# A scanned early-fusion layer on one core: pixel norm moved behind the embedding, text feed-forward blocks split over two loop bodies, feed-forward weights prepared ahead of the scan

## The chip, the cores and the metric

One core of a Trainium2 chip. The metric is the device time of one execution, in microseconds, as the median of several runs. Before: 1290.85 us, median of 3 runs (1287.31 to 1292.6). Engines are named as the profile names them: PE (TensorE), DVE (VectorE), ACT (ScalarE), POOL (GpSimd), SP (SyncE, which here only issues DMAs).

## The reference, cut to what matters

```python
h = tok(x)                 # 32 images, 14x14 patches of 16x16x3 -> 256: pixel layernorm with gain and
                           # bias, @ W (768x256) + bias, layernorm with gain and bias
h = concatenate([h, txt])  # 196 + 77 = 273 tokens of 256, batch 32
# scan over every second token (TIMESCALE = 2), D = 256, S = 64
x_sub = rmsnorm(layernorm(h)[:, ::2]) * g_norm
x_proj, gate = split(x_sub @ w_in.T + b_in)
def step(s, xt):
    s = tanh(s * A + xt[:, :, None] * Bm)      # s: 32 x 256 x 64
    return s, s @ Cm.sum(0) + Dv * xt
attn = (scan(step, x_proj) * silu(gate)) @ w_out.T + b_out
h = h + repeat(attn, 2)
f = layernorm(h)
h = h + (silu(f @ wg.T) * (f @ wu.T)) @ wd.T   # int weights / 127, hidden 768
```

## The kernel before

**Tiling.** The 273 tokens are cut into 20 groups of 14 rows (one row of patches, or 14 text tokens; the last has 7): 14 image groups, then 6 text groups. A group gives 7 scan steps (4 in the last). The state of the scan (256 x 64 per batch element, 32 elements) is held as 8 chunks of 128 x 512 in a ring `h`. So a group is 56 slots of one chunk each: DVE grows the chunk (`grow`, L829: old state times A into one of four PSUM banks `U`), PE adds the input (`drive`, L1384, with weights `b_st` and moving `x_diag`), ACT takes the tanh back into `h` (`squash`, L1097). In a slot the growth waits for the squash four slots earlier. After each step PE sums the state into `Y` (`read_step`, L1394).

**Bodies.** One loop body `i` does five things at once, of five groups: loads and normalises the pixels of group `r = i+1` (`ahead`), embeds, normalises and projects group `g = i` (`pre`), scans `s = i-1` (`scan`), takes `q = i-2` through attention output, residual and the feed-forward blocks (`post`), and does the down projection and output of `d = i-3` (`down`). Bodies -1 to 2 are unrolled, 3 to 12 are a loop of image bodies, 13 is the last image body, 14 to 18 a loop of text bodies, 19 the last one, 20 to 22 are the tail: body 20 has the last 32 scan slots.

**Order.** Each engine runs its own stream. What it does beside the scan is written out by hand in `PLANS`: for each kind of body, each part has the slot behind whose growth, drive or squash it stands, on the engine that does it. Within a slot the order is that of the code. POOL has its own list, `POOL_ORDER`. SP issues in the order of `sync_body`: next pixels (`load_raw`), gate in, y out to DRAM and back in another layout, text in, output stores, wait for those stores, `res` in, the late half of `x_diag` (steps 4 to 6), token store, `x_hi` and `x_lo` out to `scan_scr`, the early half of `x_diag` for the next body, gate out.

**Parts that the change touches.** Pixel norm: `raw_patch` (L836, 14 statistics), `raw_means` (L842), `average` (L1413, means over the three colour channels by PE), `raw_deviation` (L847 to L853), `raw_variance`, `raw_rsqrt` on POOL (L1260), `raw_shift` (L863), then 14 normalisations of 96 x 256 into `rawn`, 7 on ACT (L1113) and 7 on POOL (L1292), one body ahead. `turn` (L1443) transposes `rawn`, `xT_copy` (L1121) evicts, `embed` (L1460) multiplies by `tok_w`, `tok_stats` (L907) adds the bias. Input of the scan: `x_copy` (L1169, L1174) gives `xf` and `x_hi`, `x_low_part` (L953, on DVE) gives `x_lo`. Residual: `residual` (L963) adds attention to `res`, `finish` (L999) adds the down projection to `res` in place; the output is stored from `res`. Feed-forward: six hidden blocks, each `ffn` gate and up (L1564, L1565), `ffn_silu` (L1201), `ffn_product` (L988), `act_high_part` (L1206), `act_low_part` on POOL (L1313); `shrink` (L1580, L1581) is the down projection. Weights: `ffn_cast` (L554), `ffn_max` (L559), `ffn_turn` (L578) and its evictions, all in the body in which the scan starts. `clear_stage` (L459) and `clear_rest` (L499) clear the tile that `x_diag` shares with the setup.

## Time and profile before

| | |
|---|---|
| median of 3 runs | 1290.85 us |
| the profiled execution, whole | 1288.43 us |
| its span, first to last instruction | 1286.7 us |
| PE busy | 1193.1 us (93%) |
| DVE busy | 1078.1 us (84%) |
| ACT busy | 982.7 us (76%) |
| POOL busy | 434.3 us (34%) |
| granted PE clock, mean | 0.982 |

Times in the views are microseconds from the start of the span. "L829" is line 829 of the kernel before. In the timeline a row is a run of equal instructions on one engine: start, time from the first start to the last end, engine, line, operation, output and inputs, shapes, count, and in brackets how long the engine stood idle before and what released it. Two instructions in a row overlap by some 0.1 us on DVE and ACT, so the cost of one is the distance between starts. PE ends are modelled: there too only the distance between starts counts. In the table of stages each stretch has its length, then busy time and instructions of each engine, the granted PE clock (1.00 is full), the busy share of the DMA engines and what they moved.

### The profile page before, as it was taken

The numbers are of one execution on the slowest core, as the hardware profiler recorded it, in microseconds if no ns is written. First come the engines' busy times: TensorE is split into PE (matmuls) and PEld (weight loads), VectorE is DVE, ScalarE is ACT, GpSimd is POOL, SyncE is SP. The second block draws the span as 40 slices with busy tenths as digits, with TensorE's granted clock in tenths as the row PEclk, the third lists the DMA queues.
The fourth block names the chain that finished last, engine by engine and source line by source line (L and its number), as shares of the span: only waits on it lengthen the run. The fifth ranks groups of instructions, "written<-read, shape, count | busy, mean of one in ns | idle before, by whom it ended". The sixth has DMA issues, their size and how long they took to land.

```text
span 1286.7 us, 26087 instructions
## 1 busy us (share of the span) xinstructions
PE 1193.1 (93%) x7217; PEld 643.8 (50%) x7217; DVE 1078.1 (84%) x2423; ACT 982.7 (76%) x1944; POOL 434.3 (34%) x435
## 2 busy tenths in 40 slices
PE   6788999999999999999999999999999999999987
PEld 4543546464646464646464646464444444444435
DVE  4898988898989898989898989878989889888843
ACT  2358796979797979797979797978888787787852
POOL 6522252525252525252525252514132121321320
PEclk8879899999999999999999999999999999999989
DMA  7423233232323232323232323222322323322210
GB/s 168 129 50 87 58 83 76 71 88 68 89 70 87 71 86 70 87 71 85 70 87 71 85 72 85 65 50 67 93 73 78 96 61 85 85 73 65 66 50 23
DMA packets 154815, 99.60 MB, mean 77 GB/s; under 512 B 129073, under 2 KB 143537, under 8 KB 153425
## 3 DMA queue, kind: packets, MB, share of 16 engines
q1 hardware_dynamic: 151120, 97.58, 29.8%
q10 hardware_dynamic: 3648, 1.46, 0.5%
q8 instruction: 23, 0.38, 0.1%
q14 instruction: 24, 0.19, 0.0%
HBM read 58.39 MB, written 40.60 MB: 77 GB/s over the span
## 4 chain that ended last, share of the span: by engine, by line
PE 46%; DVE 16%; issue 14%; ACT 11%; DMA 5%; POOL 3%; SPq 2%; DVEq 1%; ACTq 0%; POOLq 0%
PE Y L1394 11%; PE U L1384 9%; DVE U L829 7%; PE P L1460 7%; ACT h L1097 5%; PE P L1564 5%; PE P L1565 4%; DMA raw<-in_x 3%; PE P L1580 2%; PE P L1581 2%; PE P L1443 2%; PE P L1495 2%; DMA y_scr<-y_fx 1%; PE P L1515 1%; ACT fsg L1201 1%
## 5 line engine op out<-in xcount | busy, mean ns | idle before, releaser
L829 DVE TENSOR_TENSOR U<-h,a_col 128x512 f32<-128x512 f32 x1096 | 708.2, 689 | 85.6 <-ACT h L1097 81.1
L1097 ACT ACTIVATE h<-U 128x512 f32<-128x512 f32 x1096 | 611.1, 609 | 155.6 <-PE U L1384 150.5
L1384 PE MATMUL U<-x_diag,b_st 128*128 128x512 f16 x1096 | 368.7, 383 | 42.6 <-DVE U L829 40.1
L1394 PE MATMUL Y<-h,read_st 128*32 128x512 f32 x2192 | 266.8, 605 | 5.9 <-ACT h L1097 5.9
L1384 PEld LDWEIGHTS U<-x_diag,b_st 128*128 128x128 f16 x1096 | 101.3, 98 | 210.9 <-DVE U L829 153.5
L1313 POOL TENSOR_TENSOR xT_act<-act,xT_act 128x448 f16<-128x448 f32 x114 | 117.9, 1038 | 157.0 <-ACT xT_act L1206 157.0
L1460 PE MATMUL P<-tok_w,xT_act 128*112 128x256 f32 x648 | 160.6, 381 | 0.1
L1460 PEld LDWEIGHTS P<-tok_w,xT_act 128*112 128x112 f32 x648 | 113.1, 177 | 41.4 <-ACT xT_act L1121 10.1
L1394 PEld LDWEIGHTS Y<-h,read_st 128*32 128x32 f32 x2192 | 57.5, 109 | 134.2 <-issue 106.4
L1580 PE MATMUL P<-down_w,xT_act 128*112 128x256 bf16 (+1 forms) x480 | 114.6, 275 | 2.3 <-DVE xT_act L1006 1.6
L1581 PE MATMUL P<-down_w,xT_act 128*112 128x256 bf16 (+1 forms) x480 | 114.4, 275 | 0.0
L988 DVE SCALAR_TENSOR_TENSOR act<-fsg,P 128x448 f32<-128x448 f32 (+1 forms) x118 | 72.1, 612 | 40.9 <-PE P L1565 38.7
L1271 POOL TENSOR_TENSOR yT<-yT,gate_in 128x448 f32<-128x448 f32 x20 | 22.8, 1142 | 226.3 <-DMA yT<-y_scr 226.3
L1121 ACT ACTIVATE xT_act<-P 128x384 f32<-128x384 f32 x108 | 80.0, 798 | 20.9 <-PE P L1443 18.8
L1260 POOL TENSOR_TENSOR res_s<-res_s,half_th 112x4 f32<-112x4 f32 x20 | 20.6, 1028 | 204.6 <-DVE res_s L977 204.6
L1564 PE MATMUL P<-fx_split,up_w 128*128 128x448 f16 (+1 forms) x236 | 83.1, 353 | 2.1
L1564 PE MATMUL P<-fx_split,gate_w 128*128 128x448 f16 x228 | 81.3, 356 | 3.0 <-DVE fx_split L994 1.9
L1565 PE MATMUL P<-fx_split,up_w 128*128 128x448 f16 (+1 forms) x236 | 82.6, 352 | 0.0
L1565 PE MATMUL P<-fx_split,gate_w 128*128 128x448 f16 x228 | 80.9, 355 | 0.0
L836 DVE BATCH_NORM_STATS2 raw_st<-raw 96x6 f32<-96x256 f32 x196 | 71.8, 410 | 9.9 <-DMA raw<-in_x 9.7
L1495 PE MATMUL P<-xaT,in_w 128*128 128x224 f32 x320 | 77.5, 369 | 1.3 <-ACT xf L1169 0.8
L1201 ACT ACTIVATE fsg<-P 128x448 f32<-128x448 f32 x114 | 63.4, 556 | 14.5 <-PE P L1565 13.2
(165 smaller groups left out, 1514.3 us busy)
## 6 DMA issues: line engine op xcount, KB each, us to landing
raw<-in_x SPq DMA_DIRECT2D x42, 448.0 KB, 6.2
gate_scr<-gate_o SPq DMA_DIRECT2D x20, 448.0 KB, 2.5
gate_in<-gate_scr SPq DMA_DIRECT2D x20, 448.0 KB, 7.8
tok_scr<-tok SPq DMA_DIRECT2D x19, 448.0 KB, 3.2
res<-tok_scr SPq DMA_DIRECT2D x19, 448.0 KB, 3.7
out<-res SPq DMA_DIRECT2D x76, 112.0 KB, 2.3
x_diag<-scan_scr SPq DMA_DIRECT2D x312, 16.0 KB
x_diag<-scan_scr SPq DMA_DIRECT2D x304, 12.0 KB
```

The source lines that it names most:

```text
L829: dve.tensor_tensor(U[bank_of(slot)][:, :].rearrange("p (l b) -> p l b", b=B), h[:, (slot - CHUNKS) % RING, :].rearrange("p (l b) -> p l b ...
L1097: sc.activation(h[:, slot % RING, :], U[bank_of(slot)][:, :], ACT.Tanh, scale=1.0 / U_SCALE).then_inc(squashed, 1)
L1121: sc.activation(xT[:, hf * CH:hf * CH + CH, par, :].rearrange("p c (b t) -> p t c b", t=STEPS)[:, t0:t0 + nt], P[turn_bank(n)][:, 0:nt * R ...
L1313: gp.tensor_tensor(act_lo[:, k, :], act[:, k, :], act_hi[:, k, :], ALU.subtract).then_inc(act_lo_done, 1)
L1384: pe.matmul(U[bank_of(slot)][:, :], b_st[:, c, :], x_diag[:, c, :, t * B:t * B + B], start=False, stop=True, skip_group_check=True).then_i ...
L1394: mm = pe.matmul(Y[c4 * 32:c4 * 32 + 32, :], read_st[:, t, half, :], h[:, (t * CHUNKS + half * RG + c4) % RING, :], start=(t == 0 and half ...
L1460: mm = pe.matmul(tok_bank(k // 2, g)[0:PT, (k % 2) * D:(k % 2) * D + D], xT[:, f, k // 2, (k % 2) * PT:(k % 2) * PT + PT], tok_w[:, f, :], ...
L1495: mm = pe.matmul(P[1][:, k * TOK:k * TOK + TOK], in_w[:, j, e0:e0 + 128], xaT[:, j, :], start=(j == 0), stop=(j == DB - 1))
L1564: pe.matmul(bank, half, fx_hi[:, j, 0:n], start=(j == 0), stop=False)
L1565: mm = pe.matmul(bank, half, fx_lo[:, j, 0:n], start=False, stop=(j == DB - 1))
L1580: pe.matmul(bank, act_hi[:, f, k * m:k * m + m], half, start=(f == 0), stop=False)
L1581: mm = pe.matmul(bank, act_lo[:, f, k * m:k * m + m], half, start=False, stop=(f == HB - 1))
```

## The change

- **Output buffer.** `finish` reads `res` and writes a new tile `outs`, which is stored. `res` of the next group is loaded as soon as both parts of `finish` are done, ahead of the output stores; `finish` waits for the stores of one body earlier.
- **Late text blocks.** In text bodies (from body 15) and in body 20, the last two of the six feed-forward blocks of group `q` are computed in the next body, in slots 0 to 9 (`late_gate`, `late_up`, `late_silu`, `late_product`, `late_high`, `late_low`).
- **Pixel norm behind the embedding.** ACT (3 instructions) and POOL (2) copy the raw pixels into patch order without normalising. `tok_w` becomes gain times W less its column mean, by 12 more matmul records and a different scaling in the setup. The statistics are averaged in the body of the embedding, brought into token layout by two matmuls, a multiplication by a 0/1 pattern and a reduction, and `tok_stats` multiplies the embedding by the inverse deviation as it adds the bias.
- **x_lo.** `xf` is scaled once, `x_hi` is a copy, `x_lo` a subtraction on POOL (on DVE for group 0).
- **Weights.** Casts, maxima, transposes and evictions of the feed-forward weights and the split of `b_out` move from body 1 to body 0, ahead of the first drive. Their loads are issued ahead of the second pixel load. `clear_stage` moves from slot 11 to slot 52 of body 0.
- **Orders.** All lists of `PLANS` and `POOL_ORDER` are new.

```diff
 PLANS = {
     "image": dict(
-        read=(0, 12, 18, 29, 33, 42, 51), shrink=(2, 2, 4, 5, 6, 6, 8, 8), turn=(8, 9, 10, 10, 11, 12, 13, 16),
-        attend=(16, 16), average=(18, 20), embed=(18, 19, 19, 20, 21, 22, 24, 24, 26, 27, 28, 28), turn_fx=(31,
...
-        ffn_silu=(35, 36, 37, 39, 49, 53), act_high_part=(36, 46, 48, 50, 53, 55),
-        normalise=(28, 28, 28, 29, 42, 47, 49), residual=(19,)),
+        raw_patch=(13, 13, 14, 15, 18, 19, 22, 31, 32, 39, 40, 42, 42, 43), raw_means=(44,), sort_low=(42, 45,
+        53), read=(2, 13, 18, 29, 32, 42, 53), shrink=(0, 1, 4, 6, 7, 8, 8, 9), turn=(9, 11, 12, 14, 16, 17, 18,
+        22), attend=(22, 22), average=(23, 24), embed=(23, 23, 23, 24, 25, 25, 26, 26, 27, 27, 28, 28),
+        turn_fx=(31, 31), ffn_gate=(34, 36, 38, 40, 43, 49), ffn_up=(34, 39, 42, 44, 49, 52), turn_xa=(36,),
+        project=(40, 40, 47, 47), finish=(10, 12), raw_deviation=(25,), raw_variance=(26,), res_stats=(24,),
...
     "text": dict(
-        read=(0, 13, 21, 29, 36, 41, 53), shrink=(3, 4, 6, 8, 10, 15, 19, 20), attend=(23, 24), turn_fx=(39,
-        39), ffn_gate=(43, 45, 46, 48, 50, 51), ffn_up=(44, 45, 46, 48, 50, 51), turn_xa=(26,), project=(28, 28,
...
+        shrink=(12, 12, 14, 15, 17, 18, 19, 19), finish=(22, 23), ffn_gate=(37, 40, 43, 49), ffn_up=(38, 41, 46,
+        50), ffn_silu=(37, 40, 45, 50), ffn_product=(41, 48, 50, 54), act_high_part=(43, 46, 49, 52),
+        late_gate=(0, 4), late_up=(4, 7), late_silu=(0, 3), late_product=(7, 9), late_high=(7, 8), read=(1, 8,
+        21, 28, 34, 45, 52), attend=(24, 24), turn_fx=(31, 32), turn_xa=(26,), project=(27, 27, 30, 30),
+        res_stats=(28,), res_variance=(28,), res_shift=(30,), fx_low_part=(35, 37), ln_stats=(24,),
+        ln_shift=(26,), y_copy=(1,), fx_apply=(28, 28, 29, 30), fxT_copy=(31, 33), ln_apply=(24,),
...
     "first": dict(
+        sort_low=(10, 49, 55), average=(0, 3), raw_deviation=(14,), raw_variance=(17,), raw_patch=(26, 26, 36,
+        37, 37, 37, 39, 39, 49, 52, 52, 53, 53, 54), raw_means=(55,), ffn_cast=(15, 16, 19, 24, 24),
+        ffn_max=(19, 20, 28, 41, 42, 52), ffn_turn=(19, 20, 24, 24, 31, 37, 38, 38, 43, 47, 47), ffn_even=(19,
+        23, 28, 36, 37, 53), ffn_odd=(26, 36, 38, 44, 53), count_large=(47,), flag_large=(52,), bias_split=(1,
+        2, 5, 8, 12, 14, 42, 46, 54), col_scale=(3,), turn=(0, 0, 0, 0, 0, 0, 0, 0), embed=(0, 2, 5, 7, 10, 15,
...
+        x_low_first=(42,), gate_silu=(55,), clear_banks=(55,), sum_c=(53,), read_scale=(55,), b_split=(0, 2, 3,
+        5, 7, 14), c_pair=(9,), clear_stage=(52,), diag_half=(55,), keep_busy=(52, 54, 55)),
...
     "zero": dict(
+        sort_low=(7, 20, 42), gain_mean=(17,), column_mean=(15, 18, 21, 25, 34, 42), tok_scale=(25, 25, 31, 38,
+        44, 46), raw_patch=(0, 5, 7, 9, 10, 10, 10, 11, 11, 11, 13, 14, 16, 22), raw_means=(22,), bias_part=(50,
+        50, 54, 55, 55, 55), bias_add=(49,), keep_busy=(0, 0, 4)),
 POOL_ORDER = {
     "image": (
+        ("gating", 0), ("sort_high", 0), ("res_rsqrt", 0), ("raw_rsqrt", 0), ("token_rsqrt", 0), ("token_tiles",
+        0), ("ln_rsqrt", 0), ("token_rsqrt", 1), ("token_tiles", 1), ("act_low_part", 0), ("x_low_part", 0),
+        ("sort_high", 1), ("act_low_part", 1), ("skip_term", 0), ("act_low_part", 2), ("act_low_part", 3),
...
         def setup_sync(sp):
...
-            load_raw(sp, 1)
             for where, w, k0, n in ffn_r:
...
+            sp.wait_ge(raw_stats, ROW)
+            sp.sem_inc(passed, 1)
+            sp.wait_ge(sorted_low, len(ACT_SETS))
+            sp.sem_inc(passed, 1)
+            sp.wait_ge(sorted_high, len(POOL_SETS))
+            sp.sem_inc(passed, 1)
+            load_raw(sp, 1)
...
             if ahead and due(i):
-                sp.wait_ge(norm_even, r * STEPS)
+                sp.wait_ge(raw_stats, r * ROW)
...
+                sp.wait_ge(sorted_low, r * len(ACT_SETS))
...
+                sp.wait_ge(sorted_high, r * len(POOL_SETS))
                 sp.sem_inc(passed, 1)
                 load_raw(sp, r)
...
+            if post and scan:
+                if down:
+                    sp.wait_ge(out_done, d * 2 + 2)
+                    sp.sem_inc(passed, 1)
+                sp.wait_ge(tok_wr, (q + 1) * 16)
+                sp.sem_inc(passed, 1)
+                sp.dma_start(res[:, :, :], tok_scr[q]).then_inc(res_ld, 16)
             if down:
...
-                            sp.dma_start(dst[pair][hf * 16:hf * 16 + 16], res[:, k, :]).then_inc(stored, 16)
-            if post and scan:
-                if due(q * 64):
-                    sp.wait_ge(stored, q * 64)
...
+                            sp.dma_start(dst[pair][hf * 16:hf * 16 + 16], outs[:, k, :]).then_inc(stored, 16)
...
+            dve.scalar_tensor_tensor(tok_w[:, f, :], w_st[:, f, :], g1[:, f:f + 1], U[2][:, 0:D], ALU.mult, ALU.subtract)\
+                .then_inc(s_tokw, 1)
...
+        def column_mean(pe, f):
...
+            mm = pe.matmul(U[2][:, 0:D], g_mean[:, f:f + 1].to_broadcast([128, 128]), w_st[:, f, :],
+                           start=(f == 0), stop=(f == KF - 1))
...
             def tok_stats(pair):
+                dve.wait_ge(raw_rstd, g + 1)
...
-                    dve.tensor_tensor(tok[:, pair * 2 + k, :], tok_bank(pair, g)[0:PT, k * D:k * D + D], rows[:, 0, :], ALU.add)\
+                    dve.scalar_tensor_tensor(tok[:, pair * 2 + k, :], tok_bank(pair, g)[0:PT, k * D:k * D + D],
+                                             raw_t[:, 1, pair * 2 + k:pair * 2 + k + 1], rows[:, 0, :], ALU.mult, ALU.add)\
...
             def finish(pair):
                 dve.wait_ge(down_ps, d * 2 + pair + 1)
+                if not in_place and due(d):
+                    dve.wait_ge(stored, d * 64)
...
+            def sort_low(n):
...
+                sc.activation(by_patch(rawn, w0, w1), raw[:, :, w0:w1, :], ACT.Copy).then_inc(sorted_low, 1)
...
+            def sort_high(n):
...
+                if due(r):
+                    gp.wait_ge(turned_ps, r * 8)
+                gp.sem_inc(passed, 1)
+                gp.tensor_copy(by_patch(rawn, w0, w1), raw[:, :, w0:w1, :]).then_inc(sorted_high, 1)
...
+            def x_low_part():
+                gp.wait_ge(x_hi_done, g + 1)
...
+                gp.tensor_tensor(x_lo[:, :, :], xf[:, :, :], x_hi[:, :, :], ALU.subtract).then_inc(x_lo_done, 1)
...
+                if late:
+                    for k in parts_at(plan, "late_gate", slot):
+                        ffn(HB - LATE + k, 0, d)
+                    for k in parts_at(plan, "late_up", slot):
+                        ffn(HB - LATE + k, 1, d)
```

## Rows read from the trace of the kernel before

**Rows 1.** The page: span, busy tenths of PE in 40 slices, the chain by engine.
```profile
span 1286.7 us, 26087 instructions
...
PE   6788999999999999999999999999999999999987
...
PE 46%; DVE 16%; issue 14%; ACT 11%; DMA 5%; POOL 3%; SPq 2%; DVEq 1%; ACTq 0%; POOLq 0%
```

**Rows 2.** Busy time by stage (stretch, length, engines, clock, DMA), cut at first growths.
```profile
62.20:123.20 61.00, 52.41 (x286) 26.43 (x286) 56.98 (x133) 44.80 (x87) 17.56 (x21) 0.89 0.23 58
...
188.40:254.80 66.40, 62.26 (x381) 34.43 (x381) 56.53 (x136) 53.03 (x105) 25.36 (x27) 1.00 0.31 78
511.80:575.90 64.10, 61.65 (x381) 34.57 (x381) 56.26 (x135) 52.91 (x105) 25.22 (x27) 1.00 0.32 79
...
896.20:946.30 50.10, 47.48 (x291) 22.98 (x295) 45.22 (x86) 41.63 (x85) 12.34 (x13) 1.00 0.35 96
997.90:1049.40 51.50, 48.88 (x305) 23.22 (x301) 45.30 (x85) 41.98 (x86) 11.70 (x13) 1.00 0.30 79
...
1205.30:1228.70 23.40, 23.12 (x160) 11.46 (x156) 20.91 (x36) 17.48 (x34) 3.65 (x4) 1.00 0.33 90
```

**Rows 3.** Timeline of the image body from 447.6, rows that price one instruction.
```profile
464.91 2.10 ACT L1097 ACTIVATE h<-U 128x512 f32<-128x512 f32 x4
...
482.70 1.92 PE L1394 MATMUL Y<-h,read_st 128*32 128x512 f32 x16
484.55 0.61 PE L1384 MATMUL U<-x_diag,b_st 128*128 128x512 f16 x2
...
503.59 3.08 DVE L829 TENSOR_TENSOR U<-h,a_col 128x512 f32<-128x512 f32 x5
```

**Rows 4.** Timeline around x_lo in an image body, and x_lo in a text body.
```profile
498.86 0.55 POOL L1292 TENSOR_SCALAR rawn<-raw,raw_s 96x256 f32<-96x256 f32 x1
499.38 1.04 POOL L1313 TENSOR_TENSOR xT_act<-act,xT_act 128x448 f16<-128x448 f32 x1
...
499.01 1.89 DVE L953 SCALAR_TENSOR_TENSOR x_lo<-xf,x_hi 128x448 f16<-128x448 f32 x1 [0.65 <-ACT x_hi L1174]
...
501.56 0.39 PE L1384 MATMUL U<-x_diag,b_st 128*128 128x512 f16 x1 [0.88 <-DVE U L829]
...
981.04 0.62 DVE L953 SCALAR_TENSOR_TENSOR x_lo<-xf,x_hi 128x448 f16<-128x448 f32 x1
```

**Rows 5.** Chain that ended last (start, length, what), in the body from 188.4.
```profile
205.01 2.25 DMA out<-res
...
207.49 4.23 DMA res<-tok_scr
211.74 1.24 DVE res L963
```

**Rows 6.** Timeline of the head, by engine.
```profile
22.94 0.55 PE L1443 MATMUL P<-cst,rawn 96*128 96x96 f32 x4
...
33.13 2.30 DVE L459 MEMSET x_diag<- 128x2688 int32 x1 [0.49 <-issue]
...
35.94 0.74 DVE L907 TENSOR_TENSOR tok<-U,rows 112x256 f32<-112x256 f32 x2
...
55.57 3.26 DVE L554 CAST act<-act 128x1536 f32<-128x1536 int32 x2
...
55.61 2.78 SPq L812 DMA_DIRECT2D x_diag<-scan_scr  x8
...
62.15 0.38 PE L1384 MATMUL U<-x_diag,b_st 128*128 128x512 f16 x1 [1.28 <-DMA x_diag<-scan_scr]
```

**Rows 7.** Timeline at the end of an image body: x_lo, its loads, next drive.
```profile
563.19 1.90 DVE L953 SCALAR_TENSOR_TENSOR x_lo<-xf,x_hi 128x448 f16<-128x448 f32 x1 [0.65 <-ACT x_hi L1174]
...
567.94 5.51 SPq L812 DMA_DIRECT2D x_diag<-scan_scr  x16
...
576.69 0.39 PE L1384 MATMUL U<-x_diag,b_st 128*128 128x512 f16 x1 [0.89 <-DVE U L829]
```

More of the change, by code:

```diff
@@ L148 @@
     "zero": (
[L149 to L150 removed]
+        ("sort_high", 0), ("sort_high", 1)),
 }
@@ L1087, in vector_body, with scalar_body @@
                         act_low_part(k)
-        def scalar_body(sc, i, image, ahead, pre, scan, post, down, steps):
+                if late:
+                    for k in parts_at(plan, "late_product", slot):
+                        ffn_product(HB - LATE + k, d)
+        def scalar_body(sc, i, image, ahead, pre, scan, post, down, steps, late=False):
             r, g, s, q, d = i + 1, i, i - 1, i - 2, i - 3
```

373 lines of the change are left out of this document (183 added, 190 removed).

## The prediction

> **What bounds the kernel now.** I read the page first: TensorE is busy in nine tenths of nearly every slice, and the chain that ended last is 46% PE, 16% DVE and 11% ACT, mixed [rows 1]. No single engine is the bound, so the next view is busy time by stage, cut at the first growth of each body [rows 2]. There the reader sees the kinds of stage: behind a head of 62.2 us with no scan, one slow first scan body (61.0 us from its first drive), image bodies of 64.2 us and text bodies of 51.6 us, then a tail. Most of the time is twelve image bodies (123.2 to 896.2, 773 us) and six text bodies (896.2 to 1205.3, 309 us).
>
> Inside a body the three engines go in step. A slot is growth (DVE), drive (PE), squash (ACT), and only four PSUM banks are in flight, so an engine that is late by more than a few slots stops the others. I priced the orders from start to start: growth 0.60 us (five in 3.08), squash 0.49 (four in 2.10), one read 1.85 (482.70 to 484.55) [rows 3]; a drive is 0.215, an embed part 0.86, a gate or up block 0.75, each from start to next start in the same timelines. Summed over an image body PE has 58.6 us, DVE 54.6, ACT 49.8; over a text body 45.5, 44.9, 39.5. The difference to 64.2 and 51.6 is idle time from bad moments, not from too much work. To see the moments, I added the parts listed for each scan step (eight slots) and took the largest engine of each step. Image before: 7.6, 9.5, 11.2, 9.9, 9.3, 8.9, 7.7 = 64.1, measured 64.2. Text before: 5.6, 5.6, 6.4, 7.9, 9.5, 8.1, 8.1 = 51.2, measured 51.6. So the sum by steps is a usable ruler; cut half a step later it gives 60.5 and 48.3, which shows how loose it is.
>
> **The change part by part.** The sum is against the profiled execution, 1288.4 us (span 1286.7), which is 2.4 us under the median of 1290.85.
>
> Image bodies. DVE loses x_lo. It cost 1.89 us beside a GpSimd operation and 0.62 in text bodies where GpSimd is still; behind it the next growth is late and PE stands 0.88 us [rows 4]. DVE also loses the copy and the shift of the pixel norm and gains a reduction, about nothing. ACT sorts in three instructions what it normalised in seven (7 x 0.48 = 3.4 us against some 2.05 by size). GpSimd gains x_lo (as act_low, 1.04 us [rows 4]) and has two copies for seven normalisations; it is busy 25 of 64 us [rows 2], so that is covered, at most 1.3 us of delay for x_lo if act_low is in front. PE has the same work. By the step ruler, after: 6.9, 7.3, 9.5, 12.2, 10.1, 9.6, 6.5 = 62.1. The half step cut gives 62.3, no gain, so I take 62.6, that is 1.6 less for a plain body. The body from 188.4 took 66.4: its output stores land, then res is loaded for 4.23 us, then the residual starts [rows 5]. With a buffer of its own the load starts when finish is done, before the stores; this body falls to 62.6 too. Sum: first image body behind the start 65.2 to 63.2 (-2.0), this one -3.8, the nine from 254.8 to 833.1 together 578.3 to 563.4 (-14.9), the last (833.1 to 896.2) 63.1 to 62.0 (-1.1): -21.8 us.
>
> Text bodies. Two of six blocks go to the start of the next body, where before PE and DVE had only the scan (first steps 5.6 and 5.6). After, by steps: 6.6, 6.3, 6.3, 9.8, 5.9, 6.6, 6.4 = 47.9. The y copy also waits no longer for a read in its own slot. Against that stand the late silu orders in slots 0 and 3, ahead of the squash while PE makes the gate in slots 0 and 4; I give them 0.9 us a body and take 48.8 (-2.8). The res load again has to wait for finish (slot 23) and takes 3.7 to 4.2 us [rows 5] to the residual in slot 28, so at most 1 us of DVE waiting is left, inside those 0.9. Four plain bodies -11.2, the last 52.7 to 49.8 (-2.9), the first (50.1 [rows 2], no late blocks yet, four own) to 47.0 (-3.1): -17.2. The two late blocks land in the short scan of the last body: its four steps go from 22.1 to 25.5, +3.4 on the 23.4 of [rows 2]. In the tail the last y copy stood behind two silus and a high part; it now stands behind one silu, but the feed-forward chain beside it ends almost as late: -1.5, between -3 and 0.
>
> Head. In before the turns start at 22.94, the first token statistics at 35.94, the loads of x_diag at 55.61 and the first drive at 62.15 [rows 6]. The raw norm no longer stands before the turns, but column means and bias (24 matmul records, 8.9 us at the 0.37 each that the bias takes before) do, from about 14.4 when the gain mean comes: turns again at about 23. Then DVE gets new work ahead of the first drive: casts (3.26 for two of five [rows 6], 5.3 in all), maxima 5.4, five evictions of 0.42, nine small bias steps 3.5. Of these the casts and two maxima (8 us) stand ahead of the first token statistics, some of it in time that DVE stood waiting there; the statistics start at about 41.5, 5.6 later. The clearing (2.30 us [rows 6]) was at 33.1, far ahead; in the new order it comes behind x_lo and most maxima, at about 61 to 63.5, and only then may x_diag be loaded (6.5 us from first issue to drive, 55.61 to 62.15). First drive at about 69.5: +7.4, between 0 and +15. The first scan body loses all of this DVE work and 26 turns: 61.0 to about 50.5 (ruler 49.1, plus 1.4 for a start at granted clock 0.89 [rows 2]): -10.5. Together -3.1.
>
> Sum: -21.8 - 17.2 + 3.4 - 1.5 - 3.1 = -40.2, so 1248.2; forecast 1248 us.
>
> A wait is added on SP: the next raw load also waits for the sort in slot 53, and the gate load and y stores are queued behind it. They are due 3 slots later; covered. finish waits for stores a body old; covered.
>
> The Trainium skill, "SBUF — State Buffer", section "Who interferes with whom", says that a DVE instruction with two SBUF inputs and a GpSimd instruction reading SBUF exclude each other for the whole instruction. The trace agrees in 1.89 against 0.62 us. Read against this change, the longer GpSimd copies would stop what is left of such DVE work; rival one has its price from rows.
>
> **The rivals.** One: GpSimd's sorts take over the stall. Three windows in one copy are 3 x 0.55 = 1.6 us (one normalise is 0.55 in the GpSimd timeline [rows 4]) just when DVE does the small two-input steps of slot 25, and four windows 2.2 us near the others. Then each image body keeps its idle time and stays at 64.2; only the body at 188.4 and the start gain: images -3.0, total 1288.4 - 3.0 - 17.2 - 1.2 = 1267. For it: x_lo itself was stopped 1.3 us. Against it: growth and product run unslowed beside GpSimd.
>
> Two: the bubbles close. Then the image body is held by its early x_diag load, text by PE. x_lo's loads are issued to 573.45 and the drive comes at 576.69 [rows 7], where I count 1.3 us to spare by comparing with the first drive, so the floor is about 61.4; text 47.5. Images -35.7, text -25.1, total 1226.
>
> Three, slower: x_lo becomes late on GpSimd. From x_lo's end to the next first drive the stores and 16 loads need 10.3 us (from 565.09, x_lo's end, to 576.69 there are 11.6 [rows 7], 1.3 of them to spare). I count x_lo's end at 51.4 us of the body. If it is behind token_tiles and act_low and the port, 5 us later, the body is 66.7: +2.5 in twelve bodies, total 1288.4 + 30 - 17.2 - 1.2 = 1300. It eats the whole gain from 3.9 us of delay on. Against it: those GpSimd items are due 3 slots before.
>
> Four: the text blocks are moved in vain, the late silus stop the squash for what is won, and one holds too: text 0, images -3, total 1284, no change.
>
> Five: the head is worse by 8 us (all new DVE work is on the path): 1256, inside the range.
>
> **How the numbers follow.** Forecast (1238 to 1258) 0.52, five 0.10, one 0.15, two 0.10, three 0.07, four 0.06. Leaving out two's end, three and four gives 1229 to 1274. A measurement of this kernel tells 0.5% (6.5 us) from no change: faster than 1284 are forecast, five, one, two and a bit of four, 0.88; same 0.05; slower 0.07.
>
> **What would show it.** Image bodies 62.6 and text bodies 48.8 from first growth to first growth; no DVE x_lo and no PE gap of 0.9 us behind it; residual of the third body without a DMA wait; first drive near 69.5 and first scan body near 50.5; last scan body near 27; last y copy relatively earlier. Wrong if image bodies stay at 64 (one), if the first drive of a body waits for x_diag (three), or if the first drive comes past 77.

## The result and the profile after

The changed kernel takes 1239.13 us (median of 4, 1238.44 to 1239.38), the kernel before beside it 1291.72: ratio 0.9597, 95% interval 0.9573 to 0.9622. It was forecast at 1248 with a range of 1229 to 1274, so the time lies inside. The profiled execution of the changed kernel is 1238.44 us long, its span 1236.6 against 1286.7: 50 us were won there, where the prediction's sum had 40. Which stages gave them is another matter.

The page of the changed kernel, the same lines as [rows 1]:

```profile
span 1236.6 us, 25959 instructions
...
PE   6898999999999999999999999999999999999977
...
PE 71%; DVE 13%; ACT 6%; issue 6%; DMA 1%; SPq 1%; POOL 0%; ACTq 0%; DVEq 0%; POOLq 0%
```

The chain is now 71% TensorE, where it was 46%. Busy time by stage, with the columns of [rows 2] and cut at first growths (the first row at the first drive):

```profile
63.80:115.80 52.00, 46.73 (x254) 23.90 (x254) 45.32 (x111) 41.15 (x77) 12.68 (x13) 0.93 0.27 63
115.80:176.60 60.80, 56.87 (x330) 29.73 (x333) 53.70 (x132) 49.35 (x99) 21.09 (x21) 0.97 0.32 77
176.60:238.50 61.90, 61.30 (x387) 34.77 (x383) 55.50 (x134) 50.51 (x101) 22.12 (x22) 1.00 0.34 83
423.20:484.70 61.50, 61.11 (x387) 34.75 (x383) 55.39 (x133) 50.46 (x101) 22.11 (x22) 1.00 0.33 82
854.10:902.80 48.70, 45.60 (x292) 21.77 (x284) 43.30 (x82) 40.38 (x82) 10.90 (x11) 1.00 0.38 105
952.10:1001.40 49.30, 47.96 (x306) 23.40 (x303) 44.31 (x85) 42.02 (x86) 12.92 (x13) 1.00 0.32 84
1099.90:1151.70 51.80, 49.74 (x305) 24.31 (x301) 44.48 (x85) 41.80 (x86) 12.94 (x13) 0.97 0.27 67
1151.70:1176.50 24.80, 24.16 (x157) 12.28 (x153) 22.09 (x37) 18.98 (x37) 5.39 (x5) 1.00 0.25 60
```

The first scan body is 52.0 us (61.0 before), a plain image body 61.56 by the first growths (64.2), a plain text body 49.27 (51.59), the last text body 51.8 (52.7). An image body now shows DVE 55.39 and PE 61.11 of 61.5 us: PE stands still for 0.4 us by this view, where it stood 2.4 in [rows 2]. Against the sum of the prediction:

| stage | predicted | measured |
|---|---|---|
| head and first scan body, to 123.2 | -3.1 | -7.4 (115.8) |
| twelve image bodies, 773 us | -21.8 | -34.7 (738.3) |
| six text bodies, 309 us | -17.2 | -11.5 (297.6) |
| last body's short scan, 23.4 us | +3.4 | +1.4 (24.8) |
| tail behind the last growth, 58.0 us | -1.5 | +2.1 (60.1) |
| sum | -40.2 | -50.1 |

That the total came this close is partly luck: the image bodies gave 12.9 us more than predicted and the text bodies 5.7 less. The experiments ask where the image gain comes from, since the three edits that touch these bodies (x_lo, output buffer, norm) arrive together with a new order of slots.

### The profile page after: what moved, and what is told of

Read it like the earlier page. It is cut to its first block, busy times and chain, and to the rows that moved or that the text cites. A ratio compares the mean times of both kernels' runs of the same rounds, so it can differ in the third digit from the quotient of the medians.

```text
span 1236.6 us, 25959 instructions
## 1 busy us (share of the span) xinstructions
PE 1179.6 (95%) x7257; PEld 647.2 (52%) x7257; DVE 1057.5 (86%) x2390; ACT 953.6 (77%) x1891; POOL 393.7 (32%) x384
## 4 chain that ended last, share of the span: by engine, by line
PE 71%; DVE 13%; ACT 6%; issue 6%; DMA 1%; SPq 1%; POOL 0%; ACTq 0%; DVEq 0%; POOLq 0%
PE Y L1446 14%; PE U L1436 14%; PE P L1507 8%; PE P L1611 7%; PE P L1612 7%; PE P L1542 4%; PE P L1627 4%; PE P L1628 4%; DVE U L867 4%; PE P L1492 3%; PE P L1562 3%; ACT y_fx L1221 2%; ACT h L1134 2%; DVE act L1018 1%; DVE fx_split L1024 1%
## 5 line engine op out<-in xcount | busy, mean ns | idle before, releaser
L1436 PE MATMUL U<-x_diag,b_st 128*128 128x512 f16 x1096 | 352.8, 382 | 10.1 <-DVE U L867 7.1
L1507 PE MATMUL P<-tok_w,xT_act 128*112 128x256 f32 x648 | 155.1, 380 | 0.0
L1154 ACT ACTIVATE xT_act<-P 128x384 f32<-128x384 f32 x108 | 84.7, 798 | 13.1 <-PE P L1492 13.1
L874 DVE BATCH_NORM_STATS2 raw_st<-raw 96x6 f32<-96x256 f32 x196 | 77.9, 414 | 9.9 <-DMA raw<-in_x 9.8
L1542 PE MATMUL P<-xaT,in_w 128*128 128x224 f32 x320 | 71.4, 366 | 5.6 <-ACT xaT L1179 3.2
L1241 ACT ACTIVATE xT_act<-act 128x448 f16<-128x448 f32 (+1 forms) x120 | 69.8, 583 | 1.3 <-DVE act L1018 1.2
```

What stands on the lines that cost most here:

```text
L1154: sc.activation(xT[:, hf * CH:hf * CH + CH, par, :].rearrange("p c (b t) -> p t c b", t=STEPS)[:, t0:t0 + nt], P[turn_bank(n)][:, 0:nt * R ...
L1436: pe.matmul(U[bank_of(slot)][:, :], b_st[:, c, :], x_diag[:, c, :, t * B:t * B + B], start=False, stop=True, skip_group_check=True).then_i ...
L1507: mm = pe.matmul(tok_bank(k // 2, g)[0:PT, (k % 2) * D:(k % 2) * D + D], xT[:, f, k // 2, (k % 2) * PT:(k % 2) * PT + PT], tok_w[:, f, :], ...
L1542: mm = pe.matmul(P[1][:, k * TOK:k * TOK + TOK], in_w[:, j, e0:e0 + 128], xaT[:, j, :], start=(j == 0), stop=(j == DB - 1))
```

## The experiments

All ratios are to the kernel before on the same chip. "Body" lengths are from first growth to first growth in the profiled execution. Where one number stands, plain bodies agree within 0.03 us (for e2's text bodies from the third on; the second is 49.5). Each run has one profile, and the stretch ahead of the scan is less steady than the bodies: in the six runs whose code is the same there as in the change (e1, e2, e3, e8, e10, e12) the first growth lies between 61.5 and 63.1 us, the first drive between 62.6 and 64.3.

| kernel | us | ratio, 95% interval | plain image body | plain text body |
|---|---|---|---|---|
| before | 1290 | 1 | 64.2 to 64.6 | 51.6 |
| changed | 1239.1 | 0.9573 to 0.9622 | 61.56 | 49.27 |
| e1 no output buffer | 1278.8 | 0.9886 to 0.9937 | 61.9 to 62.7 | 53.6 to 55.2 |
| e2 x_lo on DVE | 1245.1 | 0.9638 to 0.9681 | 62.2 | 49.25 |
| e3 no late blocks | 1256.6 | 0.9715 to 0.9759 | 61.56 | 52.2 to 53.9 |
| e4 weight turns in first scan body | 1244.0 | 0.9610 to 0.9664 | 61.56 | 49.26 |
| e5 before + output buffer | 1287.4 | 0.9972 to 0.9995 | 64.2 | 51.6 |
| e6 before + x_lo on GpSimd | 1290.3 | 0.9999 to 1.0020 | 63.2 to 63.8 | 52.2 to 53.8 |
| e7 seven sorts on ACT | 1239.9 | 0.9610 to 0.9637 | 61.7 | 49.26 |
| e8 x chain later | 1254.1 | 0.9709 to 0.9747 | 62.7 to 63.0 | 49.26 |
| e9 GpSimd sorts twice | 1238.6 | 0.9593 to 0.9627 | 61.55 | 49.26 |
| e10 old slots | 1318.8 | 1.0208 to 1.0249 | 67.6 to 68.5 | 49.25 |
| e11 two mends | 1235.9 | 0.9561 to 0.9591 | 61.55 | 49.25 |
| e12 old slots, room for the norm | 1286.6 | 0.9949 to 1.0005 | 65.2 to 65.7, one 67.2 | 49.25 |

### e1: the output buffer undone

```diff
-            sum_t, out_t = (tok, tok) if in_place else (res, outs)
+            sum_t, out_t = (tok, tok) if in_place else (res, res)
...
-                            sp.dma_start(dst[pair][hf * 16:hf * 16 + 16], outs[:, k, :]).then_inc(stored, 16)
+                            sp.dma_start(dst[pair][hf * 16:hf * 16 + 16], res[:, k, :]).then_inc(stored, 16)
+            if post and scan:
+                if due(q * 64):
+                    sp.wait_ge(stored, q * 64)
...
+                sp.dma_start(res[:, :, :], tok_scr[q]).then_inc(res_ld, 16)
```

> The changed kernel with the output buffer undone: finish writes into res again, the stores leave from there, and SP loads res behind them. All else, the slots too, stays. Theory (the buffer matters where finish and residual stand close): in image bodies there are 12 slots, some 13 us, between finish and residual, enough for stores (2.25 us) and load (4.23 us), so the image bodies stay at 61.6 us, the third too. In text bodies residual comes five slots, about 4 us, behind finish; stores and load need about 8, so each of the text bodies from the second on gains some 4 us, 49.3 to about 53, total about 1239 + 20 = 1259. Rival (the slots alone did it, the stores land in time): text bodies stay at 49.3, total 1239. Second rival, as the prediction told it: the third image body gets back its 3.8 us and the rest stays, total 1243.

Measured: 1278.79 us, 40 slower than the change. What DVE waited for in front of its residual, over the whole run, first in the kernel before, then changed, then e1 (us in total, times):

```profile
  DMA res<-tok_scr: 5.3, 9
```
```profile
  PE P L1562: 9.5, 13
```
```profile
  DMA res<-tok_scr: 39.4, 17
  PE P L1560: 3.5, 3
```

That 39.4 is close to 40 is partly luck, since not every microsecond waited is lost and some of the loss is no wait. By stages the twelve image bodies lose 8.8 us, the six text bodies 27.0, the last scan and the tail 5.5, and the stretch ahead of the scan gains 1.3. In the six text bodies the waits for the load are 22.1 us; each of these bodies also has 3.4 us or more at a granted clock of 0.50, which only the last text body of the changed kernel has. Plain text bodies lose 4.3 to 5.9 us, a little more than the theory said. That plain image bodies lose 0.3 to 1.2 us was not expected; SP's own row of work shows why. An image body of e1 (start, length, what):

```profile
627.59 3.12 SPq L782 DMA_DIRECT2D out<-res  x4
632.64 0.35 SPq L789 DMA_DIRECT2D res<-tok_scr  x1
```
```profile
636.64 1.22 DVE L993 SCALAR_TENSOR_TENSOR res<-P,res 112x1024 f32<-112x1024 f32 x1 [1.72 <-DMA res<-tok_scr]
```

The two finishes run at 621.8 and 623.8, but SP issues the stores only at 627.59, behind the y loads; issuing takes 3.1 us, landing 2 more, the load 4. The 12 slots to the residual are used up mostly by a queue, not by the transfer. The theory had counted 6.5 us from finish to landing; from the second finish to the residual it is 12.8 us (623.8 to 636.6).

### e5: the output buffer alone, in the kernel before

```diff
-            out_t = tok if not scan and not post and down else res
+            in_place = not scan and not post and down
+            sum_t, out_t = (tok, tok) if in_place else (res, outs)
```
(with the load ahead of the stores, as in the change)

> The kernel before with the output buffer alone (the read weights are loaded straight to their tile to make room for it). Theory (in the old order of work the buffer can only take away the waits that are seen): DVE's residual waits 5.3 us for the res load, over nine bodies; they go, the third image body falls from 66.4 to 64.4 and others by 0.3 us, text bodies stay at 51.6: total 1290.5 - 5 = 1285. Rival (the same 40 us as undoing it costs in the changed kernel, since the queue on SP is shorter for all that follows): total 1250 to 1265.

Measured: 1287.37 us, 3 faster, ratio 0.9983. The third body falls from 66.4 to 64.8 us, plain image bodies end at 64.2 in place of 64.2 to 64.6, text stays at 51.6. The theory had the right kind of effect, a little too large: the same edit is worth 3 us in the old order (interval 0.6 to 3.6) and 40 in the new one. The new order puts residual five slots behind finish (28 and 23) in text bodies, which only the buffer allows.

### e2 and e6: x_lo's engine

e2 gives x_lo back to DVE in the changed kernel, e6 moves it to GpSimd in the kernel before:

```diff
+            def x_low_part():
+                gp.wait_ge(x_hi_done, g + 1)
...
+                gp.tensor_tensor(x_lo[:, :, :], xf[:, :, :], x_hi[:, :, :], ALU.subtract).then_inc(x_lo_done, 1)
```

> The changed kernel with x_lo on DVE again: in slot 44 of image bodies, 33 of text bodies and 43 of the first scan body. It finds xf already scaled. Theory (x_lo's place was worth its stall): x_lo takes 1.9 us beside the GpSimd work and PE stands 0.9 us behind it, so an image body goes from 61.56 to about 62.8 and a text body from 49.27 to 49.5; total about 1239 + 12 x 1.2 + 6 x 0.3 = 1255. Rival (PE's own work or the x_diag loads hold the body, and x_lo is covered): image bodies stay within 0.3 us of 61.56, total at most 1242.

> The kernel before with x_lo on GpSimd alone, ahead of the first act_low, xf scaled as in the change. Theory (as taking it back cost 0.65 us an image body and nothing in text): image bodies 64.2 to 63.5, text 51.6, total 1290.5 - 8 = 1282. Rival, as the prediction had it (PE's 0.9 us gap and the DVE stall both go): image bodies to 62.9, text by 0.3, total 1273. Second rival (nothing is won without the other slots): 1290.

Measured: e2 1245.13 us, 0.65 us more in each image body, nothing in text: half of what the theory gave. x_lo took 0.92 us there (0.62 in text bodies), beginning inside a GpSimd copy of 1.03, and PE did not stand idle behind it. e6: 1290.28 us, no change, and that hides two effects. The nine plain image bodies fall from 64.3 to 63.6 us in the mean, 5.8 us together; all twelve are 11.0 us shorter, but 4.0 of that is the first of them, whose granted clock was 0.95 before and 1.00 here. Text bodies rise from 51.6 to 52.2 or 53.8 us, all six together by 10.4 us, and give it back. The text body of e6 from 938.9 and the one before from 997.9, first DVE and GpSimd of e6:

```profile
968.77 1.29 DVE L835 TENSOR_TENSOR U<-h,a_col 128x512 f32<-128x512 f32 x2
969.97 0.98 DVE L987 SCALAR_TENSOR_TENSOR res_s<-res_mv,res_s 112x4 f32<-112x4 f32 x1
...
969.90 1.03 POOL L1341 TENSOR_TENSOR x_lo<-xf,x_hi 128x448 f16<-128x448 f32 x1
```
then DVE of the kernel before:
```profile
1028.95 0.16 DVE L981 SCALAR_TENSOR_TENSOR res_s<-res_mv,res_s 112x4 f32<-112x4 f32 x1
```

An operation on 112 x 4 elements took 0.98 us in place of 0.16: it began 0.07 us behind x_lo on GpSimd and ended with it. That delays the next growth, and PE waits 1.1 us where it waited 0.3. In some bodies more follows. The text body from 991.1 of e6 (columns as in [rows 2]; the clock stands third from the right):

```profile
1023.10:1025.10 2.00, 1.05 (x6) 0.35 (x10) 1.92 (x4) 1.89 (x4) 0.06 (x1) 1.00 0.44 113
1025.10:1027.10 2.00, 2.00 (x16) 0.44 (x8) 1.80 (x3) 2.00 (x5) 0.00 (x0) 0.50 0.08 16
1027.10:1029.10 2.00, 2.00 (x13) 0.57 (x6) 0.09 (x1) 0.53 (x2) 0.00 (x0) 0.65 0.27 46
```

PE is busy for half of two microseconds, then its granted clock is 0.50, that is 1.2 GHz, for 3.4 us, and the body is 53.8 us long and not 52.2. The next body, 52.2 us long, has the same half idle stretch, and its clock stays at 1.00:

```profile
1076.92:1078.92 2.00, 1.05 (x6) 0.35 (x10) 1.92 (x4) 1.89 (x4) 0.06 (x1) 1.00 0.44 113
```

Why it falls in one turn of the loop and not in the next stays open. In the changed kernel x_lo starts at 980.31, behind the same small operation (980.00, 0.16 us), so the order avoids it.

### e3: no late blocks

```diff
-        LATE_TEXT = dict(TEXT, late=True)
+        LATE_TEXT = TEXT
```
(text and last orders of the kernel before, x_lo on GpSimd)

> The changed kernel with no text blocks moved to the next body: the text and last orders are those of the kernel before, only x_lo stays on GpSimd. Theory (the late blocks gave the text gain): text bodies 51.0 us, the last scan body back to 23.4, total about 1239 + 11.5 - 0.8 + 1 = 1251. Rival (the gain came from x_lo leaving DVE or from the other slots): text bodies at 49.5, total 1240.

Measured: 1256.60 us, 17 more than the change, theory 12. Text bodies are 52.24 us with full clock and 53.6 to 53.9 (last 55.8) with a dip:

```profile
903.70:957.56 53.86, 50.47 (x305) 23.49 (x301) 45.61 (x85) 42.34 (x86) 12.79 (x14) 0.97 0.30 79
957.56:1009.80 52.24, 48.83 (x305) 23.23 (x301) 45.62 (x85) 42.21 (x86) 12.81 (x14) 1.00 0.30 78
```

The late blocks, together with the order that goes with them, are thus worth 3.0 us a body against this order. Of the loss, 0.6 us and the dips are those of e6: the same 0.98 us operation stands here (934.80), which leaves the 2.3 us by which text bodies are shorter than before the change. The edit takes back blocks and slots at once, and no run has the new slots without the late blocks, so how much of the 2.3 us each gives is not shown. The last short scan takes the late blocks for 1.4 us (24.1 us from first to last growth against 22.7).

### e4: the eleven weight turns back in the first scan body

```diff
-        ... ffn_turn=(19, 20, 24, 24, 31, 37, 38, 38, 43, 47, 47), ffn_even=(19,
+        ... ffn_turn=(31, 36, 39, 40, 41, 45, 48, 49, 51, 53, 55), ffn_even=(31, 38, 44, 46, 51, 55),
```
(from the order "first" to "second", into bank P[0])

> The changed kernel with the eleven feed-forward weight turns and their evictions (6 on ACT, 5 on DVE) back in the first scan body; casts, maxima and bias steps stay ahead of the scan. Theory (PE work is free ahead of the scan and is not in the first scan body): the first drive comes 2 us earlier (63.75 to about 62), and the first scan body gets the turns' PE time, 52.0 to about 58; total about 1239 + 4 = 1243. Rival (the head pays as much for the turns as the scan body saves): first drive 58 to 59, total 1239.

Measured: 1243.98 us. The first growth is at 63.64 and the first drive at 64.81, no earlier than with the turns (62.69 and 63.75 in the change, 61.5 to 63.1 and 62.6 to 64.3 in the others). The first scan body is 57.0 us from growth to growth against 53.1:

```profile
63.64:120.67 57.03, 50.63 (x293) 27.12 (x290) 48.67 (x119) 45.40 (x87) 12.66 (x13) 0.97 0.31 76
```

The total is as the theory had it, though the intervals of e4 and of the change overlap, so what is shown are the 4 us of the one body. The split is not as the theory had it: ahead of the scan the turns cost nothing that shows above the spread there.

### e7 and e9: is the image body held by ACT or GpSimd?

```diff
-ACT_SETS = ((0, 2), (2, 4), (4, 7))
+ACT_SETS = ((0, 1), (1, 2), (2, 3), (3, 4), (4, 5), (5, 6), (6, 7))
```
and, for e9,
```diff
+                gp.tensor_copy(by_patch(rawn, w0, w1), raw[:, :, w0:w1, :]).then_inc(sorted_once, 1)
+                gp.wait_ge(sorted_once, r * len(POOL_SETS) + n + 1)
                 gp.tensor_copy(by_patch(rawn, w0, w1), raw[:, :, w0:w1, :]).then_inc(sorted_high, 1)
```

> The changed kernel with ACT's three sorting copies cut into seven of one window each, in the same slots, so ACT has some 1.3 us more in an image body (7 x 0.48 against 2.1). Theory (part of the image gain is ACT's shorter work): image bodies from 61.56 to about 62.1, total about 1239 + 6 = 1245. Rival (PE is the bound, ACT is covered): within 0.2 us of 61.56, total at most 1241.

> The changed kernel with GpSimd's two sorting copies made twice each (the second waits for the first), so GpSimd has 1.9 us more in each image body. It tests the prediction's rival one. Theory (seen in the DVE timelines: a small DVE operation with two SBUF inputs that starts beside a GpSimd operation lasts as long as that one, but few stand where the sorts are): image bodies from 61.56 to at most 61.9, mostly from act_low being later, total 1239 to 1243. Rival one (the sorts stop DVE for their whole length): 1.9 us more in each image body, total about 1239 + 22 = 1261.

Measured: e7 1239.94 us, 0.14 us more a body. A plain image body of the change and one of e7:

```profile
484.73:546.30 61.57, 61.17 (x387) 34.75 (x383) 55.45 (x133) 50.52 (x101) 22.13 (x22) 1.00 0.33 82
483.42:545.12 61.70, 61.24 (x387) 34.72 (x383) 55.39 (x134) 50.72 (x105) 22.12 (x22) 1.00 0.33 82
```

The edit was much weaker than its expectation reckoned. Sorts of one window in a row overlap: the seven keep ACT busy for 2.49 us where the three took 2.12, and all of ACT's work rises from 50.52 to 50.72 us. So ACT got 0.2 to 0.4 us more and not 1.3, and the body grew by a third to two thirds of that. In e9 1.85 us more on GpSimd cost nothing, 1238.59 us. A plain image body of e9:

```profile
544.90:606.50 61.60, 61.22 (x387) 34.77 (x383) 55.52 (x134) 50.53 (x101) 23.96 (x24) 1.00 0.33 82
```

GpSimd is no hold in the new order, and rival one of the prediction falls there. ACT is not excluded: e7 is too small for that. The exclusion of e6 is real, but in this order nothing of DVE that it would stop stands on the path where the sorts are. In the old order it does, as e12 shows below.

### e8: is it held by the early x_diag loads?

```diff
-        ... project=(40, 40, 47, 47) ... x_copy=(40,)
+        ... project=(41, 41, 47, 47) ... x_copy=(42,)
```

> The changed kernel with the projection one slot later and the x copies two slots later (42 for 40) in image bodies, so x_hi, x_lo, their stores and the sixteen early x_diag loads come 1.5 to 2 us later. Theory (the chain of x_lo, stores and loads stands right before the first drive, with 0.8 to 1.0 us from its last packet): an image body grows by 1 to 2 us, 61.56 to about 63, total about 1239 + 16 = 1255. Rival (TensorE's own work holds the body, the loads have slack of 2 us): 61.6 to 61.9, total at most 1242.

Measured: 1254.12 us, 1.17 us more a body, as the theory of the loads said. The place says otherwise. The bodies' lengths by scan step (eight growths each, summed from the growths' starts):

```
              steps 1 to 7                                 sum
changed       7.28  7.49  6.75 12.88 11.11  9.23  6.83    61.56
e8            7.28  7.49  6.76 12.88 11.11 10.39  6.83    62.73
```

All of it is in the sixth step, slots 40 to 47, and none where the loads end. There PE waits in front of an up block:

```profile
480.11 0.35 PE L1611 MATMUL P<-fx_split,up_w 128*128 128x448 f16 x1 [0.66 <-ACT xf L1204]
```

The projection lies in the bank that the up block takes next, so a late x_copy stops PE at once. The last packet of the early loads comes 0.46 to 0.67 us ahead of the first drive in e8 (0.76 to 0.99 in the change), and the drive stands right behind PE's matmul before it. The loads are not what holds the body, at a distance of some tenths of a microsecond; by how much they could come later was not tried apart from this.

### e10 and e12: the old order of the image bodies

```diff
-        raw_patch=(13, 13, 14, 15, 18, 19, 22, 31, 32, 39, 40, 42, 42, 43), raw_means=(44,), sort_low=(42, 45, 53), ...
+        read=(0, 12, 18, 29, 33, 42, 51), shrink=(2, 2, 4, 5, 6, 6, 8, 8), turn=(8, 9, 10, 10, 11, 12, 13, 16),
+        attend=(16, 16), average=(20, 22), embed=(18, 19, 19, 20, 21, 22, 24, 24, 26, 27, 28, 28), turn_fx=(31, 32), ...
```
(e12: average 19 and 22, raw_deviation 24, raw_variance 25, tok_stats 27)

> The changed kernel with the image bodies' order of the kernel before: every part that both kernels have stands in its old slot, the sorts stand where the first, fifth and last normalisation of ACT stood, x_lo on GpSimd ahead of act_low, the statistics' averages in slots 20 and 22. Parts that the change removed stay removed. Theory (the last 2 us of the image gain, 63.6 with x_lo alone moved to 61.56, come from the new order that the edits made room for): image bodies 63.3 us, total about 1239 + 12 x 1.7 = 1260. Rival (the pixel norm's work off DVE and ACT is itself the gain, whatever the order): image bodies 61.6 to 62.0, total 1239 to 1244.

> The same old order of the image bodies again, but with room for the norm's new chain, which stood 3.94 us on DVE behind TensorE's average in the run before: average in slots 19 and 22, deviation in 24, variance in 25, first token statistics in 27 with their shift and normalise one slot later. Theory (the parts that the change moved off DVE and ACT give little by themselves, the new order that they allow gives the rest): with the 3.94 us wait and the clock dip behind it gone, image bodies 63.3 to 64 us, total 1260 to 1270. Rival (the removed norm work is the gain, and only the chain's place spoiled the last run): 61.6 to 62.3 us, total 1239 to 1248. A third outcome, over 65 us, would say that the new chain doesn't fit the old order at all.

Measured: e10 1318.75 us, image bodies of 67.6 to 68.5, worse than before the change. My own places for the norm's chain were bad:

```profile
621.35 0.17 DVE L885 TENSOR_TENSOR raw_s<-raw_mv,P 96x14 f32<-96x14 f32 x1 [3.94 <-PE P L1459]
```

DVE asks for the average 3.94 us before PE has come to it, and in seven of the plain bodies the granted clock then falls to 0.50 for 3.4 us. e12 gives it more room; of the wait before this operation one of 1.4 us is left, in the first scan body. It takes 1286.62 us, ratio 0.9977: its image bodies, 1.3 us longer than those of the kernel before (the one of 67.2 has a fall of the clock), eat what head and text bodies keep of the change. One of them:

```profile
574.79:640.40 65.61, 61.73 (x383) 34.96 (x383) 55.59 (x133) 50.96 (x101) 22.46 (x23) 1.00 0.32 77
```

Here PE, DVE, ACT and GpSimd do the work of the changed kernel, in 65.6 us and not in 61.56. Neither the theory's number came nor the rival's, but the third outcome, over 65 us. The expectation read it as the norm's new chain not fitting the old order; the rows of this body name three places, and two of them are not that chain:

```profile
604.36 0.19 DVE L894 SCALAR_TENSOR_TENSOR raw_pick<-P,cst 112x28 f32<-112x28 f32 x1 [0.91 <-PE P L1464]
...
586.71 0.47 PE L1492 MATMUL P<-cst,rawn 96*128 96x96 f32 x3 [1.10 <-DVE outs L1031]
...
616.75 0.82 POOL L1335 COPY rawn<-raw 96x768 f32<-96x768 f32 x1
617.14 1.45 DVE L1024 TENSOR_TENSOR fx_split<-fxT,fx_split 128x448 f16<-128x448 f32 x2
618.65 0.36 PE L1611 MATMUL P<-fx_split,gate_w 128*128 128x448 f16 x1 [0.91 <-DVE fx_split L1024]
```

The chain's second average is still late for DVE by 0.91 us, 12.0 us over the run. PE stands 1.10 us in front of a transpose behind `finish`. And GpSimd's sort holds `fx_split` on DVE: the first of the two takes 0.92 us in every image body but the last (0.62 in the changed kernel), and PE stands 0.91 us in front of the first gate. That is the kind of stall that rival one had in mind, in an order that lets the two meet. A third placement could do better, since both were set by hand, so the 4 us between e12 and the change are an upper bound of what the order gives. Against e6, which has the old norm and 63.6 us, it is 2; how those 2 us divide between the norm's and ACT's shorter work and the order stays open.

### e11: a faster version

```diff
-        ... clear_stage=(52,)
+        ... clear_stage=(43,)
...
+            if last_pre:
...
+                for n in range(AHEAD_TXT):
+                    for hf in range(2):
+                        sp.dma_start(tok[n // 2:n // 2 + 15 * LAST_STEPS + 1:LAST_STEPS, (n % 2) * 2 + hf, :],
...
```

The last text body of the changed kernel is longer than its neighbours. Its timeline (SP, DVE, PE):

```profile
1109.68 9.87 SPq L764 DMA_DIRECT2D tok<-in_txt  x14
...
1121.02 0.75 DVE L968 BATCH_NORM_STATS2 ln_st<-tok 112x6 f32<-112x256 f32 x2 [1.48 <-DMA tok<-in_txt]
...
1126.06 3.25 PE L1542 MATMUL P<-xaT,in_w 128*128 128x224 f32 x8 [0.42 <-ACT xaT L1179]
```
and the clock in it:
```profile
1126.00:1128.00 2.00, 1.95 (x6) 1.75 (x7) 1.81 (x9) 1.47 (x4) 0.00 (x0) 0.55 0.24 36
```

Fourteen small loads are issued in 9.87 us, where the other text bodies issue four in 2.98; DVE waits 1.48 us for them, PE becomes idle, and eight matmuls take 3.25 us at a granted clock of 0.55 where the same eight take 1.68 us in an earlier text body (at 981.08), at full clock.

> The changed kernel with two small mends. In the last text body (the nineteenth from the first growth) six of its fourteen small text loads are issued at its start, ahead of the y stores, since DVE waits 1.48 us for them and TensorE's granted clock then falls to 0.55. And ahead of the scan the clearing of the staging area stands directly behind x_lo, not after the maxima. Theory: the last text body goes from 51.8 to 49.8 us, the first drive comes about 1 us earlier (62.8), total about 1239 - 3 = 1236. Rival for the loads: they delay the y stores, and the body stays at 51 or more. Rival for the clearing: DVE's work ahead of the first growth is a full row, so what moves behind the clearing is late by as much, and the first growth stays at 62.7.

Measured: 1235.88 us, ratio 0.9576 (0.9561 to 0.9591). The body is 49.55 us; in the change it is 51.8, in the runs e4, e7, e8, e9, e10 and e12, whose code is the same there and whose clock does not fall there, 50.5 to 51.0. So the loads' mend gives 1 to 1.5 us, and 2.3 where it also spares the fall of the clock. The clearing's mend shows no gain, as its rival said: the memset is at 52.66, 3.6 us earlier, but the first growth stays at 62.71 and the first drive comes at 64.23, both within the spread of the other runs. By total time the version cannot be told from the changed kernel, whose interval overlaps; the gain is shown for the one body alone.

## Why the prediction was right or wrong

**The bound.** "No single engine is the bound, idle time from bad moments" held: the image bodies of e12 have the work of the changed ones on every engine and take 4 us longer. The ruler of step sums was good for a whole body and poor for a step. For the image body it said 6.9, 7.3, 9.5, 12.2, 10.1, 9.6, 6.5 = 62.1; measured are the 61.56 in the table of e8. Single steps are off by up to 2.8 us. The half microsecond that was added because of the half step cut was the wrong way, and the ruler itself was half a microsecond too long: 1.0 us a body, 9.3 of the 12.9 us that the image term misses over the nine plain bodies. Another 2.4 are the first image body, put at 63.2 and measured 60.8.

**x_lo.** The signs that were read as its price (1.89 us against 0.62, a PE gap of 0.88, [rows 4]) were right as rows and are too large as a price: 0.65 us a body undone in the new order, 0.6 in the old one. Its price in text, taken as nothing, is 0.6 us and a risk of the clock in the old order, nothing in the new. In the changed kernel it stands among other GpSimd work, and DVE has none of it:

```profile
474.43 1.04 POOL L1361 TENSOR_TENSOR x_lo<-xf,x_hi 128x448 f16<-128x448 f32 x1 [0.17 <-ACT x_hi L1209]
475.41 1.04 POOL L1335 COPY rawn<-raw 96x1024 f32<-96x1024 f32 x1
```

**Norm and sorts.** "About nothing" on DVE was too little: DVE's busy time fell by 0.8 us (56.26 to 55.45) although x_lo left with 1.89, so the rest of its work grew by some 1.1. On ACT the prediction had 1.35 us less for the sorts; ACT's busy time fell by 2.4 (52.91 to 50.5). e7 gave 0.2 to 0.4 us of it back and cost 0.14, so a part of the image gain may be ACT's; how much is not shown.

**The output buffer.** The third image body was predicted 3.8 us shorter and is 4.5 (66.4 to 61.9), with no DMA wait in front of residual. e5 shows that the buffer gives 1.6 of it, not the 2.2 that the prediction gives this body above the others. That at most 1 us of residual wait is left in text held too: none is seen there. What the prediction does not say is why: it prices the buffer by [rows 5] alone, as one body's trouble. It leaves out SP's queue: with the stores behind the y loads and the load behind the stores, the old way costs 4 us or more in each text body of the new order. The buffer is what makes the new order possible.

**Text bodies.** 48.8 predicted, 49.27 measured. The term that was mis-sized is the 0.9 us for the late silus: the ruler gave 47.9, so 1.4 are lost. Little of it is where the silus stand. By steps the body is 7.08, 5.93, 6.03, 9.57, 8.50, 5.33, 6.83: the first step, which has the silus, is 0.5 us over the ruler and the second 0.4 under it, and the excess is in the fifth (5.9 by the ruler). The sixth is 1.3 us shorter (6.6 by the ruler). In the fifth PE waits for ACT's normalised residual, the input of the feed-forward, which is a part of it:

```profile
983.61 0.60 PE L1582 MATMUL P<-cst,y_fx 112*128 112x112 f32 x4 [0.64 <-ACT y_fx L1221]
```

The first text body was taken at 47.0 and is 48.7; the last at 49.8 and is 51.8, by the small loads of e11, which the sum had not looked at.

**Head.** Turns at about 23: 23.17. Statistics at about 41.5: 38.90. Clearing at 61 to 63.5: 56.24 to 58.54. First drive near 69.5: 63.75. Its rows:

```profile
32.27 1.55 DVE L591 CAST act<-act 128x1536 f32<-128x1536 int32 x2
...
38.90 0.87 DVE L939 SCALAR_TENSOR_TENSOR tok<-U,raw_t,rows 112x256 f32<-112x256 f32 x2
...
56.24 2.30 DVE L484 MEMSET x_diag<- 128x2688 int32 x1 [0.77 <-issue]
```
```profile
63.75 0.38 PE L1436 MATMUL U<-x_diag,b_st 128*128 128x512 f16 x1 [0.83 <-DMA x_diag<-scan_scr]
```

The term that was mis-sized is the new DVE row: two casts take 1.55 us, not the 3.26 of [rows 6], and all five 3.0, not 5.3. And up to the first token statistics DVE is busy 23.6 us where it was 19.1, 4.6 more and not 8, while the statistics come 3.0 us later: the rest fills time in which DVE had waited. The first scan body was predicted at 50.5 from its first drive and is 52.0, with a granted clock of 0.93 in it. Both together: 4.3 us better than the sum.

**Last body and tail.** Cut at the last growth both terms look wrong (+1.4 for +3.4, +2.1 for -1.5); cut at the last drive they are +2.9 and +0.6:

```profile
1178.52 0.82 PE L1436 MATMUL U<-x_diag,b_st 128*128 128x512 f16 x3
...
1191.29 0.59 ACT L1140 ACTIVATE y_fx<-Y 128x512 f32<-128x512 f32 x1
```

The last drive is at 1178.97 (1229.71 before), so the late blocks cost 2.9 us there, near the predicted 3.4. The y copy comes 12.3 us behind it (14.4 before), 2.1 earlier as said, and the end does not: the last residual comes 29.4 us behind the last drive in both kernels, and the rest is 0.6 us longer. That the feed-forward chain beside it "ends almost as late" was the right worry; the 1.5 us should have been nought.

**The rivals.** One fell by e9 in the new order, and its price was too high: the two sorts take 0.82 and 1.04 us, not 1.6 and 2.2. Its mechanism is real, as `fx_split` in e12 shows. Two had the right number for the image body (61.4) by a wrong mechanism (e8) and a wrong text body (47.5). Three did not come: GpSimd was free and waited 0.17 us for x_hi. Four fell with the text bodies of 49.27 us. Five fell with the first drive.

## What to carry to other kernels

When a kernel's order of work is written out slot by slot, an edit and its order are one change: alone in the old order the buffer gave 3 us and x_lo nothing, all edits together made an image body in old slots (set by hand, and not the best) 1.3 us longer, and with the new order it is 2.6 us shorter. Ask of a new buffer what two steps it allows to stand closer together, and follow the queue that serves it, not only the transfer. And where an operation moves to GpSimd, look at what DVE's small two-input operations do at that moment.

## What the runs showed of the hardware

Some DVE and GpSimd operations stop each other for whole instructions. A DVE operation of 0.16 us, with both inputs in SBUF, took 0.98, ending with the GpSimd operation on 128 x 448 elements that it began beside (e6, e3). Not every pair does. The growth, whose second input lies in PSUM, takes 0.69 us in the kernel before, whether a GpSimd operation runs beside it (398 times) or none does (633 times). And in the image bodies of the changed kernel the same 0.16 us operation begins 0.06 us behind a GpSimd operation of 1.01 us on only 112 x 4 elements, and is not held:

```profile
451.45 1.01 POOL L1300 TENSOR_TENSOR raw_t<-raw_t,half_th 112x4 f32<-112x4 f32 x1
451.51 0.16 DVE L1011 SCALAR_TENSOR_TENSOR res_s<-res_mv,res_s 112x4 f32<-112x4 f32 x1 [0.22 <-POOL res_s L1300]
```

Casts with one input feel it too: two of them took 3.26 us in the kernel before [rows 6], beside GpSimd operations that were long as well (two gate operations, 1.67 us elsewhere, took 3.15), and 1.55 us in the changed kernel with GpSimd idle. GpSimd beside the casts of [rows 6]:

```profile
56.41 1.86 POOL L1308 TENSOR_TENSOR tok<-tok,rows 112x512 f32<-112x512 f32 x1
58.26 3.15 POOL L1324 TENSOR_SCALAR gate_o<-xf,cols 128x224 f32<-128x224 f32 x2
```

By the Trainium skill, "SBUF — State Buffer", section "Who interferes with whom", two-input DVE instructions contend with GpSimd's reads, casts can enter a mode that takes the shared ports, and the one that comes second blocks fully. The trace agrees in 0.98 and 3.26 us. It does not in the pair of 451.45, where both operations have their inputs in SBUF and the second is not held; why is not shown.

TensorE's granted clock can fall inside a steady loop. In e3 and e6 the same text body ran at full clock in one turn of the loop and at 1.2 GHz for 3.4 us in the next. In e6 PE was busy for 1.05 of the 2 us before, in both kinds of turn, and its longest single wait there was 1.1 us; no text body of the kernel before, without that wait, has such a fall. A stall of 0.8 us on the critical path was thus paid with 2.2 in some bodies. Of the text bodies of the changed kernel only the last does it.
